# Attention plus FP4 feed-forward on one core: u of 768 tokens moved to VectorE in the first chunk, and a head with fewer memsets, fewer zero matmuls and another split of the first q transfers

## Chip, cores and metric

One core of one Trainium2 chip runs the whole kernel. The metric is the device time of one execution in microseconds (us), the median of several runs. Engines are named PE (TensorE matmul), PEld (its weight loads), DVE (VectorE), ACT (ScalarE), POOL (GpSimd) and SP (SyncE, which here only issues DMAs).

## Reference

The input x is 2048 tokens by 128 features. Cut to what matters:

```python
x_proj = silu(x @ W1 + b1)
u, v, q, k = split(x_proj, 4)                 # 128 features each, 16 heads of 8
attn = silu(q @ k.T) / S                      # per head, S = 2048, no softmax
y = layernorm(attn @ v * u, gamma, beta) @ W2 + b2
x1 = layernorm(x + y)
h = silu(fp4(x1) @ fp4(w_gate).T) * (fp4(x1) @ fp4(w_up).T)
out = layernorm(x1 + fp4(h) @ fp4(w_down).T)
```

fp4() quantises blocks of 16 values to the E2M1 grid and back. So there are four projections with a silu, one silu on 16 x 2048 x 2048 scores, and a feed-forward part of width 352 per token.

## The kernel before

**Steps.** The queries are cut into ten chunks (six of 256 tokens, four of 128), the keys into 16 tiles of 128. A step is one chunk, one group of head slots and one tile of keys; there are 256 steps, 32 for each wide chunk and 16 for each narrow one. In a step PE makes two halves of scores (`scores`, two PSUM banks each), ACT takes the silu of each half (`attn`, 128x1024), and PE multiplies by v two steps later (`times_v`). Three pairs of PSUM banks hold scores, so PE can be up to three halves ahead of ACT; the two banks left alternate between the attention sum of the chunk and everything else.

**Jobs.** All other PE work is a list of jobs laid out by hand over the steps: `PREP_AT` holds those of the first chunk, `TILE_AT` the feed-forward of each finished token tile, `LATE_AT` the projections of q and u that later chunks need. After the scores and the times_v of a step PE does the step's job. All jobs of a stretch share one spare bank, so PE waits before each job until the one before it has been read (`wait_bank`, `wait_job`). Readers are ACT (`ACT_JOBS`) or DVE (`VEC_JOBS`); PE, ACT and DVE each do their share strictly in order. In the kernel before, the first chunk's jobs stand at steps 0 v, 2 and 3 xT, 4 k, 6 v, 7 k, 9 v, 12 u (512 tokens, silu by ACT), 14 q, 24 w2, 26 gate, 28 up, 30 down. Job w2 multiplies the centred output weights; gate, up and down transpose the quantised weights.

**DVE in the first chunk** splits k and q into three bf16 terms (`split`), clears v_pad, and quantises the three feed-forward weights (`quantise_rows`, `fp4`), with the split of q 256 between the first and the second. Then it reads jobs w2, gate, up and down, with one addition over all of x between w2 and gate (line 1143). A silu on DVE exists for gate and for late q and u (`late_read`, `late_exponent`, `late_sum`, `late_product`): 13 linked instructions on 128x256, one of them a reciprocal.

**Head.** Before step 0, PE multiplies zeros (`WARM_UP`), transposes x (job xT), makes b1 columns, projects k and q (`HEAD`), and multiplies zeros again after two of the jobs (`FILL`). q and k are cut into bf16 terms and moved by DMA into `q_stack` and `k_stack`: eight slots, of which six (`Q_TERMS`, `K_TERMS`) hold terms and two must be zero. The transfers of the first four units are shared out among SP and POOL by `SHARES`; two of the first q unit are issued by ACT (`BY_ACT`). POOL clears k_stack columns 256 to 767, 768 to 1023 and 1024 to 1279 with `zero_k`; the units from 1280 on have only their two spare slots cleared, by DMA from a tile of zeros (`zero_rows`, on SP).

Of the kernel before, what the change touches and what calls it, by code (L numbers as in the profile page):

```python
# [53 lines left out]
def build(nc, x, W1, b1, W2, b2, gamma, beta, w_gate, w_up, w_down, out):  # L54
# [44 lines left out]
    def spare_bank(at):  # L99
# [5 lines left out]
               12: ("u", 0), 14: ("q", 256), 24: ("w2", 0), 26: ("gate", 0), 28: ("up", 0), 30: ("down", 0)}  # L105
# [9 lines left out]
    for t in range(WIDE, DENSE):  # L115
# [6 lines left out]
            6: ("q", 1280), 7: ("u", 1280), 8: ("q", 1536), 9: ("u", 1536), 10: ("q", 1792), 11: ("u", 1792)}  # L122
    LW = 256
    LATE_AT = {t: BEGIN[t // 2 + 1] + (1 if t % 2 == 0 else 17 if t < WIDE else 14) for t in LATE}
# [11 lines left out]
    for t, (base, offsets) in TILE_AT.items():  # L136
# [7 lines left out]
                if kind in ("k", "q", "v", "u") or (kind == "gate" and tile is not None and tile not in BY_VEC)]  # L144
# [11 lines left out]
    with ExitStack() as ctx:  # L156
# [104 lines left out]
        FILL = {("xT", 0): (1, 7), ("xT", 256): (2, 7)}  # L261
# [31 lines left out]
        SHARES = [((0, 1, 4), (2, 5, 3)), ((4, 5), (2, 3)), ((0, 1, 4), (2, 5, 3)), ((0, 1, 4), (2, 5, 3))]  # L293

        BY_ACT = (0, 1)

        def wait_stack(eng, n):
            if n == 1:
                eng.wait_ge(stacked_by_act, 16 * len(BY_ACT))
            if n < len(SHARES):  # L300
                eng.wait_ge(stacked[n], 16 * len(SHARES[n][0]))
                eng.wait_ge(stacked_by_pool[n], 16 * len(SHARES[n][1]))
            else:

                eng.wait_ge(stacked[n], 16 * (TERMS if n == unit_no[("k", 768)] else HD))
# [11 lines left out]
        def _(sp):  # L317
# [3 lines left out]
            load_x(sp, 2)  # L321
            sp.wait_ge(stack_zeroed, 2)
# [7 lines left out]
            sp.wait_ge(k_zeroed, 3)  # L330
            stack(sp, unit_no[("k", 768)])
            sp.wait_ge(zeros_ready, 1)
# [17 lines left out]
        def _(pool):  # L350
# [6 lines left out]
            def zero_k(start, w):  # L357

                pool.memset(k_stack[:, :, start:start + w].bitcast(U32), 0).then_inc(k_zeroed, 1)
# [11 lines left out]
            zero_k(768, 256)  # L371
# [9 lines left out]
            zero_k(1024, 256)  # L381
# [93 lines left out]
        def _(pe):  # L475
# [151 lines left out]
            def job(at):  # L627
# [10 lines left out]
                elif kind == "u":  # L638
                    last = project(bank, kind, i * CH, CH)
# [99 lines left out]
        def _(act):  # L739
# [11 lines left out]
            def project(kind, c, bank):  # L751
# [4 lines left out]
                if kind == "u":  # L756
                    return silu(uT[:, c * CH:(c + 1) * CH], ps[:, bank, :], bias=b1_col[:, 0:1])
# [26 lines left out]
            def job(at):  # L784
# [5 lines left out]
                if (kind, i) == ("u", 0):  # L790
                    act.wait_ge(b1_ready, 2)
# [27 lines left out]
        def _(dve):  # L819
# [283 lines left out]

            split("k", 0)
# [23 lines left out]
            split("k", 1792)  # L1128
            dve.wait_ge(w_loaded, 16 * W_LOADS)
# [7 lines left out]
            fp4(Blocks(blocks, blocks, P, NBF, ROWS[0]), wq_ready)  # L1137

# [103 lines left out]
```

## Time and profile before

| | us |
|---|---|
| median of 3 runs | 512.57 (512.53 to 513.4) |
| the profiled execution | 512.54 |
| its span, first to last instruction | 510.4 |

| engine | busy us | share of the span | instructions |
|---|---|---|---|
| PE | 493.1 | 97% | 9110 |
| PEld | 267.5 | 52% | 9112 |
| DVE | 359.0 | 70% | 874 |
| ACT | 483.7 | 95% | 541 |
| POOL | 94.8 | 19% | 204 |

Times below are from the start of the span. Two engines are near full, so a busy share alone does not say which of them sets the pace; that is read from the distance between their instructions. Matmul ends are modelled, so starts of successive groups say more than busy time. A merged row such as "x6" gives the start of the first and the time to the end of the last. Neighbouring instructions of ACT and DVE overlap at their ends.

### The profile page before, as it was taken

Reading aid. Unit: us, or ns where it says so; the run is one execution under the profiler, and the core shown is the slowest. Engines: PE = TensorE matmul, PEld = TensorE weight load, DVE = VectorE, ACT = ScalarE, POOL = GpSimd, SP = SyncE. Lnnn points to the kernel's source line nnn. Section 1 sums busy time; section 2 is a strip of 40 time slices with the busy share of each in tenths; the row PEclk is TensorE's granted clock in tenths of the full one; section 3 lists DMA queues with packets and bytes.
Section 4 is the critical chain, followed back from the end, with each engine's and each line's share of the span. In section 5 each row is a group of like instructions: output and inputs, shape, how many; then the busy total and the mean of one; then the engine's idle time right before and its main releaser. Section 6 shows DMA issues by size and latency. Waiting matters only on the chain.

```text
span 510.4 us, 20579 instructions
## 1 busy us (share of the span) xinstructions
PE 493.1 (97%) x9110; PEld 267.5 (52%) x9112; DVE 359.0 (70%) x874; ACT 483.7 (95%) x541; POOL 94.8 (19%) x204
## 2 busy tenths in 40 slices
PE   8899999999999999999999999999999999999995
PEld 5453344444444445444444445444477777777762
DVE  7643833878879787887879788787978583435445
ACT  4899999999999999999999999999999999999940
POOL 8414001002110401113020211113030402112020
PEclk9999999999999999999999999999999999999999
DMA  4734100001000010001000010001000000000000
GB/s 129 192 92 127 32 1 3 1 3 33 8 3 1 13 28 8 1 8 34 1 8 2 8 32 8 3 2 34 7 9 4 24 19 10 9 4 10 4 8 10
DMA packets 18630, 11.88 MB, mean 23 GB/s; under 512 B 2199, under 2 KB 18206, under 8 KB 18542
## 3 DMA queue, kind: packets, MB, share of 16 engines
q1 hardware_dynamic: 17256, 8.86, 6.7%
q0 software_dynamic: 704, 1.33, 1.0%
q8 instruction: 71, 1.16, 1.0%
q10 hardware_dynamic: 582, 0.40, 0.3%
q14 instruction: 17, 0.14, 0.1%
HBM read 1.92 MB, written 1.05 MB: 6 GB/s over the span
## 4 chain that ended last, share of the span: by engine, by line
PE 48%; ACT 28%; DVE 12%; issue 10%; DMA 1%; POOL 1%; POOLq 0%; DVEq 0%; SPq 0%
PE ps L477 46%; ACT attn L741 27%; DVE xn_b L992 2%; DVE hqT_b L987 2%; PE ps L491 2%; DMA q_stack<-parts 1%; DVE gate_b L1007 1%; DVE hqT_b L985 1%; DVE xn_b L982 1%; DVE gate_b L978 1%; DVE hqT_b L989 1%; DMA gate_b<-in_L_attn_b 1%; DVE gate_b L1046 1%; POOL rstd_b L427 0%; DVE hqT_b L981 0%
## 5 line engine op out<-in xcount | busy, mean ns | idle before, releaser
L741 ACT ACTIVATE attn<-ps 128x1024 f32<-128x1024 f32 x512 | 472.6, 1176 | 1.6 <-PE ps L477 1.4
L477 PE MATMUL ps<-attn,v_pad 128*32 128x256 f32 (+1 forms) x5120 | 274.4, 341 | 0.9 <-DVE hqT_b L1065 0.2
L477 PEld LDWEIGHTS ps<-attn,v_pad 128*32 128x32 f32 x5120 | 132.2, 109 | 81.2 <-issue 36.5
L477 PE MATMUL ps<-q_stack,k_stack 64*128 64x256 bf16 (+1 forms) x2560 | 166.7, 251 | 7.1 <-DMA q_stack<-parts 1.3
L477 PEld LDWEIGHTS ps<-q_stack,k_stack 64*128 64x128 bf16 x2560 | 81.3, 94 | 114.6 <-ACT attn L741 71.1
L426 POOL TENSOR_TENSOR ve_a<-mv_a,eps_col 128x1 f32<-128x1 f32 x24 | 4.6, 191 | 192.8 <-DVE mv_a L910 192.8
L426 POOL TENSOR_TENSOR ve_b<-mv_b,eps_col 128x1 f32<-128x1 f32 x24 | 4.6, 192 | 191.3 <-DVE mv_b L910 191.3
L477 PE MATMUL ps<-zeros 128*128 128x512 bf16 x49 | 13.6, 418 | 1.4 <-DVE zeros L1082 1.2
L970 DVE COPY xqT<-ps 128x128 f32<-128x128 f32 x15 | 4.4, 292 | 13.8 <-PE ps L477 13.8
L427 POOL TENSOR_TENSOR rstd_a<-ve_a,minus_half 128x1 f32<-128x1 f32 x24 | 13.5, 564 | 1.9
L427 POOL TENSOR_TENSOR rstd_b<-ve_b,minus_half 128x1 f32<-128x1 f32 x24 | 13.5, 562 | 1.9
L477 PE MATMUL ps<-wgate_t,xqT 128*32 128x352 f32 x128 | 12.4, 460 | 0.0
L477 PE MATMUL ps<-wup_t,xqT 128*32 128x352 f32 x128 | 12.4, 459 | 0.0
L992 DVE RECIPROCAL xn_a<-hqT_a 128x352 f32<-128x352 f32 x5 | 11.8, 2354 | 0.2
L992 DVE RECIPROCAL xn_b<-hqT_b 128x352 f32<-128x352 f32 x5 | 11.8, 2353 | 0.2
L432 POOL TENSOR_SCALAR x_a<-x1p_a,mv_a,rstd_a 128x128 f32<-128x128 f32 x14 | 11.4, 813 | 1.9 <-POOL rstd_a L427 1.1
L432 POOL TENSOR_SCALAR x_b<-x1p_b,mv_b,rstd_b 128x128 f32<-128x128 f32 x14 | 11.4, 812 | 1.9 <-POOL rstd_b L427 1.1
L477 PE MATMUL ps<-xT,w_qk 128*32 128x256 f32 (+3 forms) x82 | 10.3, 421 | 0.6 <-ACT v_sb L741 0.4
L1035 DVE RECIPROCAL xn_b<-feat 128x256 f32<-128x256 f32 x6 | 10.5, 1754 | 0.2
L1035 DVE RECIPROCAL xn_a<-uT 128x256 f32<-128x256 f32 x6 | 10.5, 1753 | 0.2
L1064 DVE COPY hqT_a<-ps 128x256 f32<-128x256 f32 x8 | 3.4, 425 | 9.6 <-PE ps L491 9.6
L477 PE MATMUL ps<-wdown_t,hqT_a 128*32 128x128 f32 (+1 forms) x192 | 9.1, 275 | 0.9 <-DVE gate_b L1046 0.9
(215 smaller groups left out, 476.8 us busy)
## 6 DMA issues: line engine op xcount, KB each, us to landing
q_stack<-parts SPq DMA_DIRECT2D x44, 64.0 KB, 2.1
k_stack<-parts SPq DMA_DIRECT2D x12, 128.0 KB, 3.0
k_stack<-parts SPq DMA_DIRECT2D x15, 64.0 KB, 2.7
q_stack<-zeros SPq DMA_DIRECT2D x14, 64.0 KB, 2.7
x_sb<-in_L_attn_x SPq DMA_DIRECT2D x3, 256.0 KB, 4.5
k_stack<-parts POOLq DMA_DIRECT2D x9, 64.0 KB, 2.6
out<-x_a SPq DMA_DIRECT2D x8, 64.0 KB, 1.6
out<-x_b SPq DMA_DIRECT2D x8, 64.0 KB, 2.1
```

The lines of the kernel that those rows point to most:

```text
L426: link(pool.tensor_tensor(r.ve[:, :], r.mv[:, which, 1:2], eps_col[:, :], ALU.add))
L427: pool.tensor_tensor(r.rstd[:, which:which + 1], r.ve[:, :], minus_half[:, :], ALU.pow).then_inc(rstd_ready, 1)
L432: return pool.tensor_scalar(to, r.x1p[:, :], r.mv[:, which, 0:1], r.rstd[:, which:which + 1], ALU.subtract, ALU.mult)
L477: return pe.matmul(to, lhsT, rhs, start=start, stop=stop, skip_group_check=True)
L491: return pe.transpose(ps[0:m, bank, a:a + n], src[:, 0:m], ident[0:n, 0:n])
L741: return act.activation(to, frm, ACT.Silu, **kw)
L978: dve.tensor_scalar(y, ps[:, bank, 0:FF], -LOG2_E, Y_MAX, ALU.mult, ALU.min).then_inc(job_by_vec, 1)
L982: link(dve.scalar_tensor_tensor(out=f, in0=spare, scalar=ROUND, in1=n, op0=ALU.subtract, op1=ALU.subtract))
L985: link(dve.scalar_tensor_tensor(out=spare, in0=f, scalar=POWERS[4] / LAST, in1=f, op0=ALU.add, op1=ALU.mult))
L987: link(dve.scalar_tensor_tensor(out=spare, in0=spare, scalar=POWERS[power] / LAST, in1=f, op0=ALU.add, op1=ALU.mult))
L992: link(dve.reciprocal(f, spare))
L1035: link(dve.reciprocal(f, spare))
```

## The change

It does four things.

- u of tokens 0 to 511 is no longer one job of 512 columns with its silu on ACT at step 12. It is two jobs of 256 columns at steps 10 and 13, with the silu on DVE (new function `activate_u`, the same 13 instructions as the late ones).
- u of tokens 1792 to 2047 is no longer late job 11 in chunk 6. It is a job at step 24 of the first chunk, with the silu on DVE after the quantisation of w_down. Jobs q 256, w2, gate, up and down move to steps 15, 27, 29, 31 and 32.
- POOL no longer clears k_stack columns 768 to 1279. SP clears the two spare slots there with two DMAs (256 KB) ahead of its first transfers into the stacks. One of the two `FILL` entries goes: one 512-column multiplication by zeros after the first xT job.
- Of the first q unit ACT issues terms 0, 1 and 4 (before 0 and 1), SP 2 and 5 (before 4 and 5), POOL 3 (before 2 and 3).

```diff
     PREP_AT = {0: ("v", 1), 2: ("xT", 1280), 3: ("xT", 1792), 4: ("k", 1280), 6: ("v", 2), 7: ("k", 1792), 9: ("v", 3),
-               12: ("u", 0), 14: ("q", 256), 24: ("w2", 0), 26: ("gate", 0), 28: ("up", 0), 30: ("down", 0)}
+               10: ("u", 0), 13: ("u", 256), 15: ("q", 256), 24: ("u", 1792), 27: ("w2", 0), 29: ("gate", 0),
+               31: ("up", 0), 32: ("down", 0)}
...
-            6: ("q", 1280), 7: ("u", 1280), 8: ("q", 1536), 9: ("u", 1536), 10: ("q", 1792), 11: ("u", 1792)}
+            6: ("q", 1280), 7: ("u", 1280), 8: ("q", 1536), 9: ("u", 1536), 10: ("q", 1792)}
...
-                if kind in ("k", "q", "v", "u") or (kind == "gate" and tile is not None and tile not in BY_VEC)]
+                if kind in ("k", "q", "v") or (kind == "gate" and tile is not None and tile not in BY_VEC)]
...
-        FILL = {("xT", 0): (1, 7), ("xT", 256): (2, 7)}
+        FILL = {("xT", 256): (2, 7)}
...
-        SHARES = [((0, 1, 4), (2, 5, 3)), ((4, 5), (2, 3)), ((0, 1, 4), (2, 5, 3)), ((0, 1, 4), (2, 5, 3))]
-
-        BY_ACT = (0, 1)
+        SHARES = [((0, 1, 4), (2, 5, 3)), ((2, 5), (3,)), ((0, 1, 4), (2, 5, 3)), ((0, 1, 4), (2, 5, 3))]
+
+        BY_ACT = (0, 1, 4)
...
             load_x(sp, 2)
+            sp.wait_ge(zeros_ready, 1)
+            zero_rows(sp, unit_no[("k", 768)])
             sp.wait_ge(stack_zeroed, 2)
...
-            sp.wait_ge(k_zeroed, 3)
             stack(sp, unit_no[("k", 768)])
-            sp.wait_ge(zeros_ready, 1)
...
-            zero_k(768, 256)
...
-            zero_k(1024, 256)
...
-                if kind == "u":
-                    return silu(uT[:, c * CH:(c + 1) * CH], ps[:, bank, :], bias=b1_col[:, 0:1])
...
+            def activate_u(start):
+
+                r = ROWS[1]
+                x, n, f, spare = r.gate[:, 0:LW], r.magic[:, 0:LW], r.xn[:, 0:LW], uT[:, start:start + LW]
+                bank = wait_made("u", start, None)
+                dve.tensor_scalar(x, ps[:, bank, 0:LW], b1_col[:, 0:1], X_MIN, ALU.add, ALU.max).then_inc(job_by_vec, 1)
+                wait_taken("u", start, None)
+                link(dve.tensor_scalar(n, x, -LOG2_E, Y_MIN, ALU.mult, ALU.max))
...
+                link(dve.reciprocal(f, spare))
+                link(dve.tensor_tensor(spare, x, f, ALU.mult))
...
             split("k", 1792)
+            activate_u(0)
+            activate_u(256)
             dve.wait_ge(w_loaded, 16 * W_LOADS)
...
             fp4(Blocks(blocks, blocks, P, NBF, ROWS[0]), wq_ready)
+            activate_u(1792)
 
             bank = wait_made("w2", 0, None)
```

## Rows read from the trace of the kernel before

**Rows 1.** Page, costliest groups: busy, mean ns of one, idle before and releaser

```profile
L741 ACT ACTIVATE attn<-ps 128x1024 f32<-128x1024 f32 x512 | 472.6, 1176 | 1.6 <-PE ps L477 1.4
```

**Rows 2.** Chain of waits of the whole span: start, us, what

```profile
52.58 1.76 ACT attn L741 x2
54.39 1.78 ACT attn L741 x2
```

**Rows 3.** Timeline of the head, all engines: start, us, engine, line, operation [idle before]

```profile
3.68 0.95 POOL L359 MEMSET k_stack<- 128x1024 uint32 x1
3.92 0.78 DVE L1088 COPY magic_b<-gate_b 4x128 f32<-4x128 f32 x1 [0.37 <-DMA gate_b<-in_L_attn_b]
4.59 0.39 ACT L768 ACTIVATE xT<-ps 128x256 f32<-128x256 f32 x1 [0.32 <-PE ps L511]
...
5.67 1.91 PE L477 MATMUL ps<-xT,w_qk 128*128 128x256 f32 x4
...
7.04 0.95 POOL L359 MEMSET k_stack<- 128x1024 uint32 x1
7.27 0.86 DVE L851 CAST parts<-feat 128x256 bf16<-128x256 f32 x1 [0.67 <-ACT feat L741]
...
10.49 0.30 DVE L851 CAST parts<-feat 128x256 bf16<-128x256 f32 x1
...
13.21 0.69 ACT L741 ACTIVATE feat<-ps,b_col 128x512 f32<-128x512 f32 x1 [0.26 <-PE ps L477]
```

**Rows 4.** Chain of waits of the first 20 us

```profile
10.91 3.24 DMA q_stack<-parts
...
14.93 2.85 ACT attn L741 x3
```

**Rows 5.** Busy time by stretch: engines, then PE clock, DMA share, GB/s

```profile
12.00:13.00 1.00, 1.00 (x4) 0.31 (x2) 0.93 (x4) 0.60 (x1) 1.00 (x3) 1.00 0.88 248
508.00:510.40 2.40, 0.00 (x0) 0.00 (x0) 0.28 (x1) 0.00 (x0) 0.00 (x0) 0.98 0.09 27
```

**Rows 6.** Timeline of ACT in the first chunk

```profile
36.59 0.59 ACT L741 ACTIVATE v_sb<-ps 128x512 f32<-128x512 f32 x1
37.07 5.64 ACT L741 ACTIVATE attn<-ps 128x1024 f32<-128x1024 f32 x6
42.61 0.68 ACT L741 ACTIVATE uT<-ps,b_col 128x512 f32<-128x512 f32 x1
43.18 3.77 ACT L741 ACTIVATE attn<-ps 128x1024 f32<-128x1024 f32 x4
```

**Rows 7.** Timeline of PE in the first chunk

```profile
30.49 0.64 PE L477 MATMUL ps<-xT,w_qk 128*32 128x256 f32 x8 [0.45 <-ACT v_sb L741]
...
67.23 0.52 PE L491 MATMUL ps<-ident,wgate_n 128*128 128x128 f32 x3
```

**Rows 8.** Timeline of DVE in the first chunk

```profile
46.69 0.42 DVE L873 TENSOR_REDUCE amax_a<-wgate_n 128x16 f32<-128x256 f32 x1 [12.23 <-DMA wdown_n<-in_L_ffn_w_down]
...
64.28 0.29 DVE L1140 TENSOR_TENSOR w_centred<-w_gamma,ps 128x128 f32<-128x128 f32 x1 [1.49 <-PE ps L477]
64.48 0.28 DVE L1141 COPY y_bias<-ps 128x128 f32<-128x128 f32 x1
```

**Rows 9.** Timeline of DVE around chunk 6, late q 1792

```profile
374.45 0.48 DVE L1007 TENSOR_SCALAR gate_b<-ps,b_col 128x256 f32<-128x256 f32 x1 [0.22 <-PE ps L477]
...
385.08 0.28 DVE L1016 TENSOR_SCALAR magic_b<-gate_b 128x256 f32<-128x256 f32 x1
...
391.27 0.51 DVE L1056 TENSOR_TENSOR gate_a<-gate_a,ps 128x352 f32<-128x352 f32 x1
```

**Rows 10.** Timeline of ACT and PE around late u 1792, chunk 6

```profile
393.27 15.10 ACT L741 ACTIVATE attn<-ps 128x1024 f32<-128x1024 f32 x16
...
397.94 0.61 PE L477 MATMUL ps<-xT,w_sb 128*32 128x256 f32 x8
...
408.55 1.94 ACT L741 ACTIVATE attn<-ps 128x1024 f32<-128x1024 f32 x2 [0.18 <-PE ps L477]
```

More of the change, by code:

```diff
@@ L121, in build @@
     LATE = {0: ("q", 512), 1: ("u", 512), 2: ("q", 768), 3: ("u", 768), 4: ("q", 1024), 5: ("u", 1024),
-            6: ("q", 1280), 7: ("u", 1280), 8: ("q", 1536), 9: ("u", 1536), 10: ("q", 1792), 11: ("u", 1792)}
+            6: ("q", 1280), 7: ("u", 1280), 8: ("q", 1536), 9: ("u", 1536), 10: ("q", 1792)}
     LW = 256
-    LATE_AT = {t: BEGIN[t // 2 + 1] + (1 if t % 2 == 0 else 17 if t < WIDE else 14) for t in LATE}
+    LATE_AT = {t: BEGIN[t // 2 + 1] + (17 if t % 2 else 1) for t in LATE}
     PARTS_AT = {}
@@ L303, in wait_stack @@
             else:
-                eng.wait_ge(stacked[n], 16 * (TERMS if n == unit_no[("k", 768)] else HD))
+                eng.wait_ge(stacked[n], 16 * HD)
         def w1_by_feature(i):
@@ L638, in job @@
                 elif kind == "u":
-                    last = project(bank, kind, i * CH, CH)
+                    last = project(bank, kind, i, LW)
                 elif kind in ("q", "k"):
@@ L789, in job @@
                 act.wait_ge(job_made, k + 1)
-                if (kind, i) == ("u", 0):
-                    act.wait_ge(b1_ready, 2)
                 if tile is None:
@@ L1102, in zero_v @@
                 dve.memset(v_pad[:, c * TPC:(c + 1) * TPC, :, :], 0.0).then_inc(v_zeroed, 1)
+            def activate_u(start):
[5 more added lines that the diff above has]
+                link(dve.tensor_scalar(n, x, -LOG2_E, Y_MIN, ALU.mult, ALU.max))
+                link(dve.tensor_scalar(spare, n, ROUND, None, ALU.add))
+                link(dve.scalar_tensor_tensor(out=f, in0=spare, scalar=ROUND, in1=n,
+                                              op0=ALU.subtract, op1=ALU.subtract))
+                link(dve.tensor_scalar(n.bitcast(U32), spare.bitcast(U32), 23, None, ALU.logical_shift_left))
+                link(dve.scalar_tensor_tensor(out=spare, in0=f, scalar=POWERS[4] / LAST, in1=f, op0=ALU.add, op1=ALU.mult))
+                for power in (3, 2, 1):
+                    link(dve.scalar_tensor_tensor(out=spare, in0=spare, scalar=POWERS[power] / LAST, in1=f,
+                                                  op0=ALU.add, op1=ALU.mult))
+                link(dve.scalar_tensor_tensor(out=spare, in0=spare, scalar=POWERS[0] / LAST, in1=n,
+                                              op0=ALU.add, op1=ALU.mult))
+                link(dve.tensor_scalar(spare, spare, LAST, 1.0, ALU.mult, ALU.add))
+                link(dve.reciprocal(f, spare))
+                link(dve.tensor_tensor(spare, x, f, ALU.mult))
             split("k", 0)
```

## The prediction

> **What bounds the kernel now.** I read the groups first. The 512 silus of scores on ACT fill nearly the whole span and ACT stood idle before them for 1.6 us in all [rows 1]. The chain of waits then gives their pace: two of them, one step, from 52.58 to 54.39, so 1.81 us a step and 0.905 us for one [rows 2]. 512 of those are 463 us. The first starts at 14.93 [rows 4], and the span is 510.4. So the time is three things: when the first silu starts, 463 us, and whatever delays a silu later: another ACT instruction, or scores that PE makes late. PE is nearly as full, but can be ahead by three halves, so it costs time only where heavy steps or a wait use that lead up. DVE costs nothing unless PE waits for it to read the spare bank. I therefore price four places: the head, the u job of step 10 to 13, the jobs of steps 24 to 32, and chunk 6.
>
> **Head, a gain.** Two POOL memsets of 0.95 us go. Beside the one at 3.68 to 4.63 a DVE copy of 4x128 takes 0.78 and ends at 4.70. Beside the one at 7.04 to 7.99 a cast takes 0.86 and ends at 8.13, while the same cast takes 0.30 at 10.49, with no memset beside it [rows 3]. Both end just behind the memset, so I read that DVE was held by it. Both lie on the way to the first scores. Without the first memset the bias copy ends near 4.1 and the small matmul that waits for it is done before PE could start on k anyway. What k then waits for is xT from ACT, ready at 4.98. With the zero matmul gone too, the four projections start at about 5.1 and not at 5.67, 0.57 earlier. The cast gives 0.56 more. So the last q term, issued at 10.91, can go at about 9.7. It took 3.24 us to land and the first silu started 0.78 after that [rows 4]. The rate bounds it as well: twelve transfers of 64 KB are 0.79 MB, which at 248 GB/s [rows 5] take 3.2 us. The first leaves near 7.1 and the last near 9.7, so at equal latency the last lands at 12.9, and at less crowding, down to about 2.4 us, at 12.1. The first silu would start at 12.9 to 13.7. Another end holds it: ACT must first finish k 768, which starts at 13.21 and takes 0.69 [rows 3], and which moves by the same 0.57 to end at 13.3. The third transfer that ACT now issues costs its queue about 0.65 us, so the k 256 silu behind it stays where it was; that slack is used, not passed on. I take 13.4 for the first silu, a gain of 1.5, less 0.1 because the x of tokens from 1280 on is loaded by SP behind transfers that move by only 0.8, and step 2 wants it 1.5 earlier. **Gain 1.4**, ends 0.4 (only the PE shift arrives) and 1.7 (all of it). The 256 KB of zeros go out at 2.7 to 3.9, behind the loads of x and ahead of the stacks; the wait for the tile of zeros is met at 1.1, so nothing queues behind it. They cost nothing as long as the DMA engines are done by 7.1; if not, up to 1 us of the gain is lost.
>
> The DMA page of the Trainium skill (DMA: Bandwidth & Descriptors, Issuing engines are not separate DMA queues) speaks against the new split of the q terms: it says that all issuers share the same 16 engines and that only issue time is saved. The DMA share of 0.88 [rows 5] agrees. By that rule the exchange itself is worth nothing but the queue's issue time, and the sum stays as it is, as it counts the earlier data alone.
>
> **u of tokens 0 to 511, a gain and a small loss.** On ACT the six silus ahead of the u silu start at 37.07 and the next one after it at 43.18: 6.11 for six, against 5.42 at the pace, so u costs 0.69 there [rows 6], 0.57 for the silu itself and the rest for PE's 512 columns. **Gain 0.69.** The new job at step 10 stands right behind v 3 of step 9, whose bank ACT frees only at 37.18 [rows 6]. The same pair stands at steps 6 and 7: the k projection starts at 30.49 after 0.45 us of waiting for v's silu [rows 7]. Here the job can start at 37.23 and is over 0.55 later, so the scores of step 11 start at 37.8. Their silu can follow about 0.44 later (an estimate: half a step's scores and their latency), at 38.24, and would have been due at 37.07 + 0.91 = 37.98, so it is 0.26 late. **Loss 0.26**, ends 0 and 0.35. The job at step 13 fits into PE's slack, about 0.7 us a step against 0.55 for it, and costs nothing.
>
> **The DVE queue up to gate, a loss.** One silu of 256 columns on DVE costs 0.52 for its read and 6.19 for the other twelve (385.08 to 391.27) [rows 9], 6.71 together. Before, DVE idles 12.23 us up to 46.69, then works without a break and waits 1.49 for w2, and the copy of y_bias at 64.48 frees the bank at 64.8 [rows 8]. Now u 0 is made at 37.23 + 0.69 (0.64 as in rows 7, and the hand-over) = 37.92, and two silus take DVE to 51.34: the idle time covers 8.77 of 13.42, and the weights start 4.65 late. The third stands ahead of the reading of w2: 6.71 more. So DVE arrives at w2 at 62.79 + 4.65 + 6.71, about 74.1, and frees the bank at 74.6. Gate is the next job, and PE waits in order, with scores and times_v queued behind it. Before, PE did gate at 67.23 at step 26 [rows 7]. Three steps later is 67.23 + 5.43 = 72.66, less 0.43 since the silus are ahead by 0.69 - 0.26: 72.23. PE waits **2.4 us** there. Its lead over ACT at that point is 0.1, so ACT loses **2.3**. The head's gain changes nothing in this, as both ends of it start from step 10. Ends 2.0 and 2.8 (the two u silus held by POOL's copies of v 3, as at 7.27 in rows 3, on the one side; silus of 6.6 on the other). Behind it, the addition over x takes DVE to about 76.9 and gate's copy to 77.4, and up, at step 31, wants the bank at 78.1 by the delayed clock: free. Down and the late jobs follow as before. Job u 1792 in the place of w2 at step 24 is shorter than it, and w2 costs at step 27 the 0.25 that it cost at step 24. The split of q 256 comes some 4.6 us late, at 58 us, and is wanted at 77.
>
> **Chunk 6, a gain.** Its 16 silus from 393.27 to 408.55 take 15.28 where the pace gives 14.48 [rows 10]: 0.8 lost. Three PE steps with a job each follow one another, the late u of 0.55 in the middle (397.94). Without it they take about 5.5 us for 5.43 of ACT. **Gain 0.48** (0.4 to 0.6); the other 0.3 hang on the chain through DVE and POOL to xqT and stay. The 6.71 us of DVE that go here buy nothing else, because DVE waits for PE there.
>
> **Sum.** 512.54 - 1.4 - 0.69 + 0.26 + 2.3 - 0.48 = 512.53, in the terms of the profiled execution, which stands 0.03 under the median. Forecast **512.5**: no change. With all ends together 511.7 to 514.3.
>
> **Rivals.** *The wait at gate is hidden.* For it: only PE waits, and DVE has 12.23 us of idle time ahead of the weights [rows 8]. Against it: the sum of DVE work is all from rows, and the job order is strict. It would need the weights to be quantised some 2.3 us faster. The time is then 510.2. Chance 0.14. *The head gains only 0.3*, because the q terms land as late as before: the added 256 KB and the third issue on ACT take back what DVE gives, or the memsets were not what held DVE. With the wait at gate in place this is 512.53 + 1.1 = 513.6, slower; it decides from a first silu later than 13.8 on. Against it are the two instructions that end with the memsets. Chance 0.15. *The clock falls at gate.* PE would stand idle for 2.4 us. In this trace the grant was still 0.98 on average in the last 2.4 us, after PE's last matmul at 506 [rows 5], so idling that long did not cost it. If it fell from 2.4 to 1.2 GHz, a PE step of 1.54 us would become 3.1 against 1.81, 1.3 us lost a step, and two such steps give 515.1. Chance 0.05. The Trainium skill (TensorE: Matmul & The Clock Gate, Why this matters for your kernels) warns of idle gaps between bursts of matmuls, and this change adds one and takes zeros away; no run here shows what a gap in mid-kernel does.
>
> **Numbers.** The forecast has 0.66. About 0.2%, 1.0 us, is what a measurement of this kernel can tell from no change. Of the 0.66, 0.56 lie within it, 0.08 are faster and 0.02 slower. The hidden wait is faster (0.14), the poor head slower (0.11) or the same (0.04), the clock slower (0.05). That is faster 0.22, same 0.60, slower 0.18. The range 511.2 to 514.0 leaves out the hidden wait and the clock.
>
> **What would show it.** In the profile after: the DVE copy at 3.9 and the cast of k 0 at 0.2 to 0.3 us each; the first silu at 13.4; no uT on ACT and 13.4 us of it on DVE from 36.5 (37.9 less the head's gain); PE idle for about 2.4 us ahead of the transposes of w_gate, with y_bias as the releaser, and one gap of 2.3 on ACT near 72; and 16 silus of chunk 6 in 14.8. If PE does not wait at gate, the forecast is wrong by the largest term. If the first silu stands at 14.5 or later, the head is.

## The result and the profile after

The kernel with the change takes **515.65 us** (median of 14 runs, 513.65 to 518.0). The kernel before, run beside it on the same chips, takes 512.55 (14 runs, 511.44 to 513.66). The ratio is **1.006, with a 95% interval of 1.0047 to 1.0072**: slower. The forecast was 512.5 with a range up to 514.0, so the prediction was wrong: it said no change, and the time lies outside its range. The profiled execution took 515.6 and its span is 513.8.

The page's engine totals and its group of silus, in the columns of [rows 1]:

```profile
PE 492.9 (96%) x9119; PEld 267.0 (52%) x9119; DVE 370.9 (72%) x900; ACT 483.4 (94%) x540; POOL 92.2 (18%) x201
...
L739 ACT ACTIVATE attn<-ps 128x1024 f32<-128x1024 f32 x512 | 473.2, 1172 | 5.5 <-PE ps L475 4.8
```

The silus cost what they cost before. ACT's idle time ahead of them is 5.5 us in place of 1.6 [rows 1], and PE released 4.8 of it. So most of the loss is scores that PE made late, and the question is where.

**The place.** The timelines of PE, DVE and ACT in the first chunk (start, us, engine, line, operation, idle before and releaser), in this order:

```profile
70.91 1.07 PE L475 MATMUL ps<-attn,v_pad 128*32 128x256 f32 x16
74.72 0.52 PE L489 MATMUL ps<-ident,wgate_n 128*128 128x128 f32 x3 [2.74 <-DVE y_bias L1160]
75.17 0.61 PE L475 MATMUL ps<-q_stack,k_stack 64*128 64x256 bf16 x8
```

```profile
37.48 0.48 DVE L1103 TENSOR_SCALAR gate_b<-ps,b_col 128x256 f32<-128x256 f32 x1 [3.49 <-PE ps L475]
...
44.48 0.48 DVE L1103 TENSOR_SCALAR gate_b<-ps,b_col 128x256 f32<-128x256 f32 x1
...
51.33 0.42 DVE L867 TENSOR_REDUCE amax_a<-wgate_n 128x16 f32<-128x256 f32 x1
...
67.34 0.48 DVE L1103 TENSOR_SCALAR gate_b<-ps,b_col 128x256 f32<-128x256 f32 x1
...
74.38 0.28 DVE L1160 COPY y_bias<-ps 128x128 f32<-128x128 f32 x1
74.70 2.29 DVE L1162 TENSOR_TENSOR x_sb<-x_sb,y_bias 128x2048 f32<-128x2048 f32 x1
```

```profile
48.09 24.99 ACT L739 ACTIVATE attn<-ps 128x1024 f32<-128x1024 f32 x27
75.61 1.94 ACT L739 ACTIVATE attn<-ps 128x1024 f32<-128x1024 f32 x2 [2.54 <-PE ps L475]
77.96 1.94 ACT L739 ACTIVATE attn<-ps 128x1024 f32<-128x1024 f32 x2 [0.41 <-PE ps L475]
80.72 3.96 ACT L739 ACTIVATE attn<-ps 128x1024 f32<-128x1024 f32 x4 [0.83 <-PE ps L475]
```

PE stands idle for 2.74 us ahead of the transposes of w_gate, with y_bias as the releaser. DVE reached y_bias at 74.38, where it was at 64.48 before [rows 8]. ACT has its gap of 2.54 right behind. This was forecast. The next two gaps were not: four silus take from 75.61 to 80.72, 5.11 us, where the pace of 0.905 gives 3.62. That is 1.5 lost, and the step behind loses another 0.2.

The reason stands in the clock column of the same stretches (busy time and count of PE, PEld, DVE, ACT, POOL, then PE clock, DMA share, GB/s):

```profile
75.00:76.00 1.00, 1.00 (x19) 0.54 (x21) 1.00 (x1) 0.39 (x1) 0.00 (x0) 1.00 0.00 0
76.00:77.00 1.00, 1.00 (x16) 0.30 (x8) 1.00 (x2) 1.00 (x2) 0.00 (x0) 0.53 0.00 0
77.00:78.00 1.00, 1.00 (x12) 0.43 (x8) 0.43 (x1) 0.59 (x2) 0.00 (x0) 0.50 0.00 0
78.00:79.00 1.00, 1.00 (x12) 0.40 (x12) 0.00 (x0) 1.00 (x2) 0.00 (x0) 0.50 0.00 0
79.00:80.00 1.00, 1.00 (x13) 0.36 (x6) 0.00 (x0) 0.90 (x1) 0.00 (x0) 0.77 0.09 16
```

PE idled from 71.98 to 74.72, worked again at full clock for over a microsecond, and was then granted 0.50, which is 1.2 GHz, until about 79.5. Its times_v group took 1.07 us at 70.91, at 2.4 GHz, and 1.66 at 75.72 in this stretch:

```profile
75.72 1.66 PE L475 MATMUL ps<-attn,v_pad 128*32 128x256 f32 x16
```

**The head.** Chain of waits of the first 16 us, then the loads and stacks by the view of DMA issues (its last number is the median time in us from issue to landing):

```profile
1.68 5.52 DMA x_sb<-in_L_attn_x
7.24 0.67 PE ps L509 x4
7.94 0.60 ACT xT L764
8.61 0.83 ACTq L775
9.46 4.11 DMA q_stack<-parts
14.03 0.41 PE ps L475 x4
14.46 1.94 ACT attn L739 x2
```

```profile
x_sb<-in_L_attn_x SPq DMA_DIRECT2D x2, 256.0 KB, 6.3
k_stack<-zeros SPq DMA_DIRECT2D x2, 128.0 KB, 6.1
q_stack<-parts ACTq DMA_DIRECT2D x3, 64.0 KB, 3.9
```

The first silu starts at 14.46 and not at the forecast 13.4; it stood at 14.93 before [rows 4]. The chain now begins with a load of x that took 5.52 us, and ends with a q term of 4.11 where the last one took 3.24 [rows 4].

**The account**, from the starts of the silus in both traces:

| place | forecast | measured |
|---|---|---|
| first silu | -1.4 | -0.47 |
| u silu leaves ACT, job at step 10 | -0.43 | -0.40 |
| w2 at step 27 | 0 | +0.15 |
| wait at gate, step 29 | +2.3 | +2.7 |
| steps 30 to 32 at half clock | 0 | +1.7 |
| chunk 5, steps 174 and 177 | 0 | +0.3 |
| chunks 6 and 7 | -0.48 | -0.50 |

These make 3.5; the last silu ends 3.37 later than before, and 0.1 is not placed. The time outside the span is 0.3 shorter, which leaves the 3.1 us between the two profiled executions. At step 174 PE waits 0.30 us for DVE's gate_a. The same 0.3 stands there in six of the nine profiled kernels that have the third u in the first chunk, and in none of those that have it in chunk 6, so it belongs to that move; how is not known.

Two theories were put to the test. **A**: the loss is the wait at gate and the fall of the clock that comes with it, and the wait exists only because both moves of u to DVE stand ahead of y_bias. **B**: the head gives back what was hoped for from it, through the zeros ahead of the stacks or the third issue on ACT.

### The profile page after: what moved, and what is told of

It is laid out like the page before. It is cut to its first block, busy times and chain, and to the rows that moved or that the text cites. A ratio compares the mean times of both kernels' runs of the same rounds, so it can differ in the third digit from the quotient of the medians.

```text
span 513.8 us, 20620 instructions
## 1 busy us (share of the span) xinstructions
PE 492.9 (96%) x9119; PEld 267.0 (52%) x9119; DVE 370.9 (72%) x900; ACT 483.4 (94%) x540; POOL 92.2 (18%) x201
## 4 chain that ended last, share of the span: by engine, by line
PE 48%; DVE 21%; ACT 20%; issue 8%; DMA 2%; POOL 1%; ACTq 0%; SPq 0%; DVEq 0%; POOLq 0%
PE ps L475 46%; ACT attn L739 19%; DVE xn_b L986 2%; PE ps L489 2%; DVE hqT_b L981 2%; DMA x_sb<-in_L_attn_x 1%; DVE xn_b L1117 1%; DMA q_stack<-parts 1%; DVE uT L1112 1%; POOL rstd_b L425 1%; DVE gate_b L1001 1%; DVE hqT_b L979 1%; DVE xn_b L976 1%; DVE hqT_b L983 1%; DVE gate_b L972 1%
## 5 line engine op out<-in xcount | busy, mean ns | idle before, releaser
L1029 DVE RECIPROCAL xn_b<-feat 128x256 f32<-128x256 f32 x6 | 10.5, 1754 | 0.2
L876 DVE SCALAR_TENSOR_TENSOR xn_b<-magic_b,xn_b 128x128 f32<-128x128 f32 (+1 forms) x16 | 9.5, 595 | 0.5
```

The costliest lines, as they stand in the source:

```text
L876: link(dve.scalar_tensor_tensor(out=t.xn, in0=t.magic, scalar=MAGIC_MIN, in1=t.xn, op0=ALU.max, op1=ALU.add))
L1029: link(dve.reciprocal(f, spare))
```

## The experiments

Ratios are to the kernel before in runs beside it (its medians there were 512.1 to 512.3), with their 95% intervals. Where a few tenths matter I give the mean span over all runs of a kernel. That of before is 509.69 to 510.07, by the group of runs that were taken side by side; a kernel is compared with the before of its own group.

**clock_held**: the kernel after, with 22 multiplications of zeros on PE while it waits at gate, added into a bank that is being filled, so nothing changes in the result.

```
                 bank = JOB_BANK[k]
+                if (kind, tile) == ("gate", None):
+                    for _ in range(22):
+                        mm(ps[:, AV[0], 0:256], zeros[:, 0:P], zeros[:, 0:256], start=False, stop=False)
                 wait_bank(at, k, bank)
```

> The kernel after, with 22 multiplications by zeros of 256 columns (start=False, so they add zero to the attention sum's bank) put ahead of PE's wait for the gate job. The wait of 2.7 us stays, but PE works through it. Theory, the wait and the clock are two costs: in the profile of after the grant was 0.50 to 0.53 from 76 to 79 us and ACT lost 1.8 us in steps 30 to 32 beyond the 2.7 at step 29. With the grant held at 1.00 these 1.8 go: 513.9 against 515.65 for after, 1.3 above before, and the runs scatter less than the 4.4 us of after. Rival, the slow scores of steps 30 to 32 are only the backlog behind the wait: 515.6 and the same gaps at a clock of 1.00.

513.86 us (7 runs), ratio 1.0034 (1.0021 to 1.0047). The timeline of PE, then the clock behind the wait:

```profile
71.98 2.58 PE L475 MATMUL ps<-zeros 128*128 128x256 bf16 x22
74.76 0.52 PE L489 MATMUL ps<-ident,wgate_n 128*128 128x128 f32 x3 [0.20 <-DVE y_bias L1163]
...
75.75 1.07 PE L475 MATMUL ps<-attn,v_pad 128*32 128x256 f32 x16
```

```profile
76.00:78.00 2.00, 2.00 (x40) 0.98 (x32) 1.46 (x2) 2.00 (x3) 0.00 (x0) 1.00 0.00 0
```

Gate begins as late as in after, so the wait and its 2.7 us on ACT stay. But the grant stays at 1.00, the same times_v group takes 1.07 and not 1.66, and the gaps of steps 30 to 32 are gone. In 6 of 7 executions the mean granted clock was 0.999 or more; the seventh had 0.992 and a span of 513.6, and where it fell is not known. Keeping PE at work through the wait is worth 1.8 us in the medians and 1.3 by the ratios. With the two groups of executions that `u_only` brings out below, this shows the clock's share of the loss.

**u1792_late**: the third u back in chunk 6, the two others on DVE.

```
-               10: ("u", 0), 13: ("u", 256), 15: ("q", 256), 24: ("u", 1792), 27: ("w2", 0), 29: ("gate", 0),
+               10: ("u", 0), 13: ("u", 256), 15: ("q", 256), 27: ("w2", 0), 29: ("gate", 0),
...
-            6: ("q", 1280), 7: ("u", 1280), 8: ("q", 1536), 9: ("u", 1536), 10: ("q", 1792)}
+            6: ("q", 1280), 7: ("u", 1280), 8: ("q", 1536), 9: ("u", 1536), 10: ("q", 1792), 11: ("u", 1792)}
...
-            activate_u(1792)
```

> The kernel after with u of tokens 1792 on back as late job 11 of chunk 6 (as in before); the jobs w2, gate, up and down stay at steps 27, 29, 31 and 32. Theory, the third silu on DVE ahead of w2 is what PE waited for: DVE frees the bank at 67.9 and not at 74.7, gate is wanted at 72, so the wait (2.7 at step 29), the slow clock behind it (1.8) and 0.15 at w2 go, and 0.5 come back in chunk 6: 515.65 - 4.7 + 0.5 = 511.5, faster than before by 1.0 (head 0.5, u silu 0.4). Rival, the two silus of u 0 and u 256 already cost PE something: 513 or more, with idle PE left between 70 and 84 us.

512.11 us (12 runs), 0.9996 (0.9981 to 1.0011): 0.6 more than expected, and level with before. The copy of y_bias and the transposes of w_gate:

```profile
69.28 0.29 DVE L1159 COPY y_bias<-ps 128x128 f32<-128x128 f32 x1
```

```profile
72.03 0.52 PE L489 MATMUL ps<-ident,wgate_n 128*128 128x128 f32 x3
```

The bank is free 2.5 us before PE wants it, and PE doesn't wait. Taking one of the three silus off DVE's queue takes the whole loss away.

**u0_by_act**: the other half. The third u early on DVE, and u of 0 to 511 on ACT at step 12 as before.

```
-               10: ("u", 0), 13: ("u", 256), 15: ("q", 256), 24: ("u", 1792), ...
+               12: ("u", 0), 15: ("q", 256), 24: ("u", 1792), ...
...
+                if kind == "u":
+                    return silu(uT[:, c * CH:(c + 1) * CH], ps[:, bank, :], bias=b1_col[:, 0:1])
...
-            activate_u(0)
-            activate_u(256)
```

> The kernel after with u of the first 512 tokens back on ACT, one job of 512 at step 12; u of tokens 1792 on stays on DVE in the first chunk ahead of w2. Theory, neither move makes PE wait by itself, their sum does: DVE then begins the weights at 46.7 less the head's gain, and frees w2's bank near 69.7, gate is wanted near 72: no wait, no slow clock. 515.65 - 4.7 + 0.4 (u silu on ACT again) = 511.35, with chunk 6 0.4 shorter than in before. Rival, the silu ahead of w2 alone makes PE wait: 513 or more and a gap at step 29.

512.11 us (12 runs), 0.9996 (0.9985 to 1.0006): 0.8 more than expected. y_bias is copied at 70.34 and gate begins at 72.11, without a wait. Chunk 6 kept its gain (29.72 us between the first silu of it and of the next, against 30.08 before), but gaps of 0.3 and 0.4 at steps 152 and 88 took it back. So **neither move makes the wait; their sum does**.

**u_only**: the moves of u and the new job order with the head of before. The reverse of `head_only`, below.

```
-        FILL = {("xT", 256): (2, 7)}
+        FILL = {("xT", 0): (1, 7), ("xT", 256): (2, 7)}
...
-            sp.wait_ge(zeros_ready, 1)
-            zero_rows(sp, unit_no[("k", 768)])
...
+            zero_k(768, 256)
...
+            zero_k(1024, 256)
```

> The kernel before with the moves of u and of the first chunk's jobs alone; head as in before. Theory, the wait at gate and the slow clock behind it are the whole loss of after: 512.3 - 0.4 - 0.5 + 0.15 + 2.7 + 1.7 = 515.95, 0.3 above after. Rival, the missing zero matmul of the head has a part in the fall of the clock at 76 us: then it does not fall here, and the time is 514.2.

514.43 us (9 runs), 1.0057 (1.0035 to 1.0080), between the two expectations, and the single runs say why. They fall into two groups: five with spans of 511.3 to 512.6 at a mean granted clock of 0.998, and four with 514.0 to 515.5 at 0.993 to 0.996. Its profiled execution is one of the first group:

```profile
74.22 0.52 PE L491 MATMUL ps<-ident,wgate_n 128*128 128x128 f32 x3 [2.71 <-DVE y_bias L1162]
...
76.76 1.07 PE L477 MATMUL ps<-attn,v_pad 128*32 128x256 f32 x16
```

```profile
76.00:77.00 1.00, 1.00 (x20) 0.47 (x16) 0.93 (x2) 1.00 (x3) 0.00 (x0) 1.00 0.00 0
```

The idle time is the same, 2.71 us, and the grant stays at 1.00. The runs of after fall apart in the same way: five of 14 with spans of 511.3 to 512.3 at 0.998 or more, nine with 513.5 to 516.2 at 0.993 to 0.996. **The wait is there in every profile of these kernels, the fall of the clock only in some executions.** The group with the lower clock is longer by 2.7 us on average in after and by 2.9 in `u_only`. Where in an execution the clock was low is known only from the profiled ones; for the others I read it from these two groups. The rival's question, whether the missing zero multiplication has a part in the fall, stays open: four of nine here against nine of 14 is too few to tell.

**wait_cut**: the kernel after with gate one step later.

```
-               ... 29: ("gate", 0),
+               ... 30: ("gate", 0),
```

> The kernel after with the gate job at step 30, not 29. PE's wait for y_bias shrinks by one step, from 2.7 to about 0.9 us. Theory, the clock falls only behind the long wait: with 0.9 us idle the grant stays at 1.00 and both the 1.8 of the wait and the 1.8 of the slow stretch go: 515.65 - 3.4 = 512.2, with 0.2 to 0.3 lost where gate, up and down follow one another. Rival, any wait there costs the clock: 513.8, with the grant at 0.5 behind step 30.

513.32 us (9 runs), 1.0029 (1.0016 to 1.0042). PE's timeline:

```profile
74.67 0.52 PE L489 MATMUL ps<-ident,wgate_n 128*128 128x128 f32 x3 [1.08 <-DVE y_bias L1160]
...
77.43 0.52 PE L489 MATMUL ps<-ident,wup_n 128*128 128x128 f32 x3 [0.70 <-DVE wgate_t L1165]
```

A miss by 1.1. The wait at gate shrank as expected to 1.08 us, but up followed one step behind and met a second wait, for gate's copy, which DVE makes only behind its addition over x of 2.29. Two jobs in neighbouring steps with that addition between them can't both be free. The mean clock was 0.997 to 1.00 in all 9 executions, so by this measure it fell in none.

**add_later**: all of u on DVE, the head's zeros behind x, the old shares, jobs at 28, 30, 31, 32, and the addition over x behind up's copy.

```
+               24: ("u", 1792), 28: ("w2", 0), 30: ("gate", 0), 31: ("up", 0), 32: ("down", 0)}
...
             dve.tensor_copy(wup_t[:, :], ps[:, bank, 0:FF]).then_inc(job_by_vec, 1)
+            dve.tensor_tensor(x_sb[:, :, :], x_sb[:, :, :], y_bias[:, :].unsqueeze(1).broadcast_to([P, KT, D]),
+                              ALU.add)
```

> The version that the runs point to: all three silus of u on DVE, zeros behind, q terms shared as in before, jobs w2, gate, up, down at 28, 30, 31, 32, and the addition over all of x on DVE moved from ahead of the copy of gate to behind that of up. Theory: a wait of 0.3 to 0.4 at gate and as much at down, no slow clock, and 0.5 from chunk 6: 510.8, level with share_undone or just under it. Rival, the waits at gate, down and the first late q add up to over 1 us: 511.5.

511.94 us (12 runs), 1.0002 (0.9988 to 1.0017). One wait of 0.86 at gate is left and none at up, and the clock stayed at 0.997 or more in all 12. It is still a miss, by 1.1: the mean span is 510.28, 0.6 above that of before, and four of the 12 executions have spans of 511.5 to 511.7. Their cause is not known; the profiled one is of the short ones (509.0).

**gate_31**: all of u on DVE, zeros behind x, and the four jobs where DVE is ready for them.

```
+               24: ("u", 1792), 29: ("w2", 0), 31: ("gate", 0), 32: ("up", 0), 33: ("down", 0)}
...
-    LATE_AT = {t: BEGIN[t // 2 + 1] + (17 if t % 2 else 1) for t in LATE}
+    LATE_AT = {t: BEGIN[t // 2 + 1] + (17 if t % 2 else 1 if t else 2) for t in LATE}
```

> All three silus of u on DVE as in after, zeros behind, and the jobs w2, gate, up and down at steps 29, 31, 32 and 33, the first late q at 34 and not 33. Theory, gate is then wanted near 75.4 and its bank free at 74.1: no wait, and all gains stand: head 0.5, u 0.4, chunk 6 0.5, so 512.3 - 1.4 = 510.9, the fastest of all. Rival, up, down, late q and y at steps 32 to 35 follow one another and use up PE's lead: 0.5 to 1 us of gaps there, 511.6.

511.73 us (12 runs), 0.9987 (0.9974 to 1.0000), as the rival said. PE doesn't wait at gate. The three jobs and the first late q in neighbouring steps 31 to 34 cost 0.6 in steps 33 to 36. The wait can be scheduled away, but not for nothing.

**head_only**: the head of the change on the kernel before.

```
-        FILL = {("xT", 0): (1, 7), ("xT", 256): (2, 7)}
+        FILL = {("xT", 256): (2, 7)}
...
+        SHARES = [((0, 1, 4), (2, 5, 3)), ((2, 5), (3,)), ((0, 1, 4), (2, 5, 3)), ((0, 1, 4), (2, 5, 3))]
+        BY_ACT = (0, 1, 4)
...
             load_x(sp, 2)
+            sp.wait_ge(zeros_ready, 1)
+            zero_rows(sp, unit_no[("k", 768)])
...
-            zero_k(768, 256)
...
-            zero_k(1024, 256)
```

> The kernel before with only the head of after: two POOL memsets gone, 256 KB of zeros by SP ahead of the stacks, one FILL entry gone, three q terms by ACT. Theory: the first silu at 14.46 against 14.93, nothing else changes, so 0.47 less: 511.8 against 512.3. Rival, the head's gain is lost again in the first chunk, because x and the k stacks arrive no earlier: 512.3, with added gaps on ACT in steps 2 to 9.

512.09 us (12 runs), 0.9996 (0.9985 to 1.0007), mean span 509.74. Against the 509.95 of its own before that is 0.2. The head as a whole is worth 0 to 0.5 and not 1.4.

**memsets_only**: the kernel before without the two memsets; the rows of zeros come by DMA **behind** all loads of x. Shares and PE's zeros as before.

```
-                eng.wait_ge(stacked[n], 16 * (TERMS if n == unit_no[("k", 768)] else HD))
+                eng.wait_ge(stacked[n], 16 * HD)
...
-            sp.wait_ge(k_zeroed, 3)
-            stack(sp, unit_no[("k", 768)])
             sp.wait_ge(zeros_ready, 1)
+            zero_rows(sp, unit_no[("k", 768)])
+            stack(sp, unit_no[("k", 768)])
...
-            zero_k(768, 256)
...
-            zero_k(1024, 256)
```

> The kernel before without the two POOL memsets of k_stack; the two spare slots are cleared by DMA behind the loads of x 3 and 4; FILL and the shares of the q terms as in before. Theory, this is what carries the head's gain: the DVE copy at 3.9 and the cast of k 0 shrink to 0.27 and 0.29 and nothing delays x or the q terms: first silu 0.9 earlier than before in profiles of the same PE pace, 511.4 against 512.3. Rival, DVE was not what set the first scores: 512.1, the first silu no earlier than 14.5.

**510.71 us** (11 runs, 510.11 to 511.6), 0.9975 (0.9966 to 0.9985), mean span 508.75, and the first silu at 13.89. This is the fastest kernel of the study, 1.4 below the one before beside it in the median, 1.3 by the ratio and 0.95 in the mean span. The copy and the cast that the memsets had held take 0.27 and 0.29. That POOL itself became free earlier is a rival, but not a likely one: in before it stood idle ahead of its first transfer, waiting for that cast.

```profile
8.80 1.88 POOL L288 DMA_DIRECT2D k_stack<-parts  x3 [0.81 <-DVE parts L851]
```

Two single steps put back onto it tell what the rest of the head costs.

**zeros_ahead**: `memsets_only` with the zeros ahead of the stacks, where the change puts them.

```
             load_x(sp, 2)
+            sp.wait_ge(zeros_ready, 1)
+            zero_rows(sp, unit_no[("k", 768)])
             sp.wait_ge(stack_zeroed, 2)
```

> memsets_only with the two DMAs of zeros ahead of the first transfers into the stacks, as in after. Theory A, they delay x (7.2 and 9.1 for 6.0 and 6.7) and the first stack transfers: first silu 0.6 to 0.9 later where PE is fast in the head, none where it is slow, on average 511.2 against 510.7. Theory B, the loads of x have slack: 510.7.

511.73 us (12 runs), 0.9989 (0.9977 to 1.0001), mean span 509.6, above both expectations. DMA issues of the first 14 us, of `memsets_only` and then of `zeros_ahead`:

```profile
x_sb<-in_L_attn_x SPq DMA_DIRECT2D x2, 256.0 KB, 4.8
```

```profile
x_sb<-in_L_attn_x SPq DMA_DIRECT2D x2, 256.0 KB, 5.4
k_stack<-zeros SPq DMA_DIRECT2D x2, 128.0 KB, 5.4
```

The loads of x stand ahead of the zeros on SP's queue and still land 0.6 later (6.3 in after). The price of the 256 KB is 0.75 us of mean span (0.95 below its before for `memsets_only`, 0.2 for `zeros_ahead`) and 0.7 by the ratios. That is about what these runs can just tell from nothing. Part of it is one execution of 511.9 with a mean clock of 0.991, and in the two profiled ones the first silu stands at 13.89 in both.

**three_by_act**: `memsets_only` with the q terms shared as in the change.

```
+        SHARES = [((0, 1, 4), (2, 5, 3)), ((2, 5), (3,)), ((0, 1, 4), (2, 5, 3)), ((0, 1, 4), (2, 5, 3))]
+        BY_ACT = (0, 1, 4)
```

> memsets_only with the q terms shared as in after: ACT 0, 1 and 4, SP 2 and 5, POOL 3. Theory A, the third issue holds ACT's queue by 0.65 us and with it the silu of k 256 and the last q term: first silu 0.4 later, 511.1 against 510.7. Theory B, the DMA engines bound the landing: no change, 510.7.

511.7 us (12 runs), 0.9989 (0.9979 to 1.0000), mean span 509.33, more than either expectation. It is 0.11% faster than before, where the memsets alone give 0.25%; in mean span, each against its own before, that is 0.5 us, again hardly more than the runs can tell. The profile doesn't show ACT's queue as the cause: ACT's third term landed at 11.84, and the last one was SP's, at 13.27.

**zeros_behind** (the kernel after with the zeros behind the loads of x), **both** (this and `u1792_late`), **share_undone** (`both` and the old shares) and **fill_kept** (`share_undone` and PE's zeros of before). The edits, in this order:

```
             load_x(sp, 2)
-            sp.wait_ge(zeros_ready, 1)
-            zero_rows(sp, unit_no[("k", 768)])
...
             load_x(sp, 4)
+            sp.wait_ge(zeros_ready, 1)
+            zero_rows(sp, unit_no[("k", 768)])
...
+        SHARES = [((0, 1, 4), (2, 5, 3)), ((4, 5), (2, 3)), ((0, 1, 4), (2, 5, 3)), ((0, 1, 4), (2, 5, 3))]
+        BY_ACT = (0, 1)
...
+        FILL = {("xT", 0): (1, 7), ("xT", 256): (2, 7)}
```

> The kernel after with the two DMAs of zeros (256 KB) issued by SP behind the loads of x 3 and 4, not ahead of the first transfers into the stacks. Theory, those 256 KB delay the loads of x (landed 7.20 and 9.10, before 6.14 and 6.90) and the first stack transfers: with them gone x lands near 6.2 and 6.9, the last q term near 12.6 (13.57) and the first silu is at 13.5 and not at 14.46: about 514.7. Rival, the third issue on ACT's queue holds the q terms: its last term is still issued at 9.5 and lands past 13.2, the first silu stays at 14.2 or later, 515.4.

> Both edits, the late u 1792 and the zeros behind. Theory, the two are independent: the sum of what they give, 515.65 - 4.2 - 1.0 = 510.5, 2 us faster than before, with the first silu at 13.5 and no gap over 0.5 us at steps 29 to 32. Rival, a stack of k is wanted earlier than the head can bring it: an added stall in steps 2 to 6 and 511.5, no faster than the late u alone.

> The kernel both (u 1792 late, zeros behind), with the q terms shared as in before: ACT 0 and 1, SP 4 and 5, POOL 2 and 3. In both and in zeros_behind the last q terms, ACT's third at 13.59 and SP's second at 13.61, landed together, 4.2 and 3.8 us after their issue. Theory A, the third issue on ACT holds the head (k 256 on ACT at 10.15 for 9.86, its own term last): without it the first silu is near 13.7, and the time 0.7 less than both, 510.7. Theory B, the 16 DMA engines are the bound (0.8 to 0.9 busy from 9 on): the first silu stays at 14.3 to 14.5 whoever issues, and the time at that of both, 511.4.

> The kernel share_undone with the FILL entry of before put back (one multiplication by zeros behind the first xT job). Theory, the 0.4 us of PE is hidden behind the xT copy on ACT (ends near 4.95): no change, 511.0. Rival A, it delays the first projection by 0.4: 511.4. Rival B, the zeros keep PE's clock up in the head (in the profile of u1792_late the grant fell to 0.50 from 7.6 to 11 us): fewer slow heads, 510.7 and less scatter.

| kernel | us | ratio | mean span | first silu |
|---|---|---|---|---|
| zeros_behind | 515.7 (5 runs) | 1.0071 (1.0057 to 1.0086) | 513.7 | 14.48 |
| both | 511.42 (11) | 0.9983 (0.9972 to 0.9994) | 508.99 | 14.39 |
| share_undone | 511.02 (12) | 0.9981 (0.9967 to 0.9995) | 509.02 | 13.98 |
| fill_kept | 511.01 (12) | 0.9982 (0.9971 to 0.9992) | 508.82 | 13.62 |

`zeros_behind` was a miss: it took nothing off. With the wait at gate still in it, the mean clock was 0.994 to 0.995 in all five of its executions, and this covers what the head gives. Its trace shows the fall at another moment than that of after. PE's timeline, then the view by stretch:

```profile
74.71 0.85 PE L489 MATMUL ps<-ident,wgate_n 128*128 128x128 f32 x3 [2.71 <-DVE y_bias L1160]
```

```profile
74.00:75.00 1.00, 0.29 (x2) 0.29 (x3) 0.93 (x4) 0.00 (x0) 0.00 (x0) 0.68 0.00 0
75.00:76.00 1.00, 1.00 (x9) 0.60 (x10) 1.00 (x1) 0.00 (x0) 0.00 (x0) 0.50 0.00 0
```

PE had been idle since 72.0. The grant fell at 74.36, within the wait, and the transposes took 0.85 for 0.52. Without the wait, in `both`, the same edit is worth 0.7 in the median against `u1792_late`. `both` was expected at 510.5 and came out at 511.42, where its rival had 511.5.

The trace of `zeros_behind` also shows why one profiled head is a poor ruler. Its x landed early, at 5.98 and 6.74, and the first silu was still at 14.48. The projections of k 0 by the timeline of PE, there and in after:

```profile
5.01 2.07 PE L475 MATMUL ps<-xT,w_qk 128*128 128x256 f32 x4
```

```profile
4.97 1.13 PE L475 MATMUL ps<-xT,w_qk 128*128 128x256 f32 x4 [0.16 <-ACT xT L764]
```

The same four took 1.91 in before [rows 3]. Over the 18 profiles they took 1.03 to 1.13 in six, 1.30 to 1.66 in four and 1.91 to 2.08 in eight. The clock events of the traces, the moments at which the grant changes, go with it: the first grant of 1.00 that a trace holds is at 3.8 to 4.9 us in the first six, at 5.9 to 6.6 in the four, and at 8.5 to 10.5 in the eight. So PE was at 2.4 GHz in this stretch in some executions and at half of that in others. This is worth close to 1 us: the profile of `u_only`, with the head of before, has its first silu at 14.00, 0.93 earlier than that of before. The 0.47 of the head in the account is therefore the difference of a head at full clock and one at half clock, and says little of the edit; the runs of `head_only` say more. `share_undone` and `fill_kept` differ by nothing that can be told: PE's zeros behind xT 0 were worth nothing either way. Undoing the shares (`share_undone` against `both`) gained 0.4 in the median and nothing in the mean span.

**late_u_early**: the fastest kernel with the third u early on DVE and u 0 on ACT, to add the gain of chunk 6 to that of the memsets. In jobs and silus it is `u0_by_act`, in the head `memsets_only`:

```
+               12: ("u", 0), 15: ("q", 256), 24: ("u", 1792), 27: ("w2", 0), 29: ("gate", 0),
...
+            activate_u(1792)
```

> memsets_only with u of tokens 1792 on moved to the first chunk, on DVE ahead of w2, jobs at 24, 27, 29, 31 and 32; u of the first 512 stays on ACT. Theory, DVE frees w2's bank near 69.5 and gate is wanted past 71: no wait, and chunks 6 and 7 are 0.5 shorter: 510.3, the fastest. Rival, as in u0_by_act small gaps of 0.3 us come up on ACT in later chunks and take the gain: 510.7.

511.67 us (12 runs), 0.9999 (0.9985 to 1.0012), mean span 509.54. A miss of both expectations. In its profile PE waits for no job of the weights in the first chunk (y_bias at 69.07, gate at 70.83), but silus come 0.3 later at steps 88 and 152. Ahead of them PE waits 0.46 and 0.44 us for DVE's xn_b; what makes DVE late there was not tried and stays open.

## Why the prediction was wrong

**The wait at gate was right, and sized a little low.** The weights began at 51.33 (51.34 said), the third silu at 67.34, and y_bias came at 74.38, with DVE said to be at w2 just before it, at 74.1. PE was at the gate 0.25 earlier than said and waited 2.74 for 2.4 forecast, ACT 2.7 for 2.3. The mis-sized term is the silu on DVE: 7.0 for the first (37.48 to 44.48) and 6.85 for the second, where 6.71 was taken. That the clock times fit to a hundredth is luck: they left out the head's gain, and it made up for the longer silus. The runs show that the wait comes from the sum of both moves: `u1792_late` and `u0_by_act` don't have it.

**The clock rival was dismissed, and it is what took the result out of the range.** The step that failed: the grant of 0.98 behind PE's last matmul [rows 5] was read as "idling that long did not cost it". The row was misread. PE's last matmul ended at 506.5, so PE idled for 3.9 us, not 2.4, up to the end of the record, and the 0.98 is an average over a fall:

```profile
510.20:510.30 0.10, 0.00 (x0) 0.00 (x0) 0.00 (x0) 0.00 (x0) 0.00 (x0) 0.96 0.00 0
510.30:510.40 0.10, 0.00 (x0) 0.00 (x0) 0.00 (x0) 0.00 (x0) 0.00 (x0) 0.50 0.00 0
```

Every one of the 18 traces ends in such a fall, 1.2 to 4.2 us behind its last matmul, so the idle time that one execution gets away with says nothing of the next. The clock was put at 0 in the sum and measured 1.7 us in the profile of after; without it the 515.6 would be 513.9, just inside the range. The mechanism of the rival was right. That its number was so near (515.1 forecast, 515.65 measured) is luck: it took 2.6 for the clock, where 1.7 came, and a head's gain of 1.4, where 0.5 came at most. Nor is the fall certain in an execution: by the mean clock it came in nine of 14 executions of after, four of nine in `u_only`, five of five in `zeros_behind`, none of nine in `wait_cut`. In mid-kernel a PE idle of 2.7 us puts the clock at risk; the one of 1.08 in `wait_cut` did not. In the head a shorter one was enough: in `u1792_late` the grant fell at 7.42, when PE had waited for x from 5.92 to 7.39. The Trainium skill (TensorE: Matmul & The Clock Gate, Why this matters for your kernels) warns of idle gaps between bursts of matmuls, though of somewhat longer ones than this; after's trace agrees that they cost the clock, with 0.50 granted from 77 to 79 behind a gap of 2.74. With the rival as the likeliest case, the forecast would have been its 515.1.

**The head was over-sized by at least three times.** The memsets did hold DVE, and this reading was right: `memsets_only` is worth 1.3 us by its ratio and 0.95 in mean span. The rest of the head took most of it back, as `head_only` keeps 0.2 of mean span. The prediction priced two terms of it at nothing. The zeros "cost nothing as long as the DMA engines are done by 7.1": they were not, the second load of x landed at 9.10 in after and at 6.90 in before, and `zeros_ahead` puts the price at about 0.75. The third issue on ACT, "slack used, not passed on": `three_by_act` puts it at 0.5, but the reverse edit in `share_undone` gained nothing in the mean span, so this price is not shown. The rival of the poor head (0.3 in place of 1.4, by the 256 KB and the third issue) had the size right, and in the zeros at least a part of the cause; its chance was 0.15. The Trainium skill (DMA: Bandwidth & Descriptors, Issuing engines are not separate DMA queues) says that issuing on several engines saves issue time only, which made the exchange of issuers worth zero in the sum. The runs agree that nothing was won by it.

**The sum's ends.** Added up from the ends that the terms have, they are 511.55 and 514.2, not 511.7 and 514.3. This changes nothing in the account.

**u of tokens 0 to 511 was right in the trace, and not seen in the times.** Steps 0 to 15 gained 0.40 for 0.43, with the stall at step 10 at 0.27 for 0.26. Yet `u1792_late` and `head_only` differ by this move and its job order alone, and both stand 0.2 below the mean span of their own before; `fill_kept` and `memsets_only` likewise, with 508.82 and 508.75. The traces place it: from the first silu to the last one, `u1792_late`, `both` and `fill_kept` take 0.34 to 0.38 less than before, `share_undone` 0.12 less, and `head_only` and `memsets_only` 0.00 and 0.06. So some 0.3 is left of the gain, and it is hidden in the scatter of the runs.

**Chunk 6 was right**: -0.50 with chunk 7, for -0.48. But the same move brought the 0.3 in chunk 5, which the sum didn't have, and is worth 0.2 net.

## What to carry to other kernels

When a change hands two pieces of work to an engine with idle time, add both to its queue up to the first thing another engine waits for: each may fit alone, and the sum not. A new wait of the tensor engine is to be priced twice, by its length and by a fall of the clock with it, which comes in some executions only; keep the wait short (the one of 1.08 us here kept its clock) or fill it with multiplications that change nothing. An average of the granted clock over a stretch can hide a fall at its end; ask for shorter stretches. Transfers that nobody waits for are better issued behind those that somebody does, also when the queue seems to put them in order already.

## What the runs showed of the hardware

- The granted clock can fall within a wait or after it. In `zeros_behind` it went from 1.00 to 0.50 at 74.36, 0.35 us before PE resumed; in after at 76.06, 1.3 us after PE had resumed. It came back 3.4 us later in both. In `u_only` the same wait (2.71) had no fall. With 22 multiplications of zeros in the wait it stayed at 1.00 in the profile of `clock_held`. What decides in which executions it falls stays open.
- In the head the view by stretch shows a clock of 1.00 for before and for after, though the same four matmuls took 1.91 in the one [rows 3] and 1.13 in the other. The traces hold no clock event ahead of 8.53 in before and of 4.38 in after, and the view shows 1.00 where there is none. A grant in the head is to be read beside the duration of a known matmul. Where the fall is recorded it looks like this, in `u1792_late`:

```profile
8.00:11.00 3.00, 3.00 (x10) 1.53 (x9) 0.77 (x4) 0.90 (x2) 1.49 (x3) 0.53 0.76 194
```

- A DVE copy and a DVE cast beside a POOL memset ended just behind the memset: 0.78 and 0.86 us [rows 3], and about a third of that without one. In the head of after the same two are:

```profile
3.84 0.27 DVE L1082 COPY magic_b<-gate_b 4x128 f32<-4x128 f32 x1 [0.29 <-DMA gate_b<-in_L_attn_b]
...
6.21 0.29 DVE L845 CAST parts<-feat 128x256 bf16<-128x256 f32 x1
```

- Loads of 256 KB that were issued first landed later (5.4 and 6.3 us, for 4.8) once 256 KB of other transfers were issued behind them on the same queue (`zeros_ahead` and after, for `memsets_only`; 4.6 in before).
